# Third attention of a four-layer gated cross-attention program: where VectorE mixes the experts' rows of tiles 3 to 7

## The chip, the core and the metric

The kernel runs on one core of one Trainium2 chip. The metric is the device time of one execution in microseconds (us), from a few executions of the same program; smaller is better. The engines of the core are TensorE (PE in the profile; its weight loads are PEld), VectorE (DVE), ScalarE (ACT), GpSimd (POOL) and SyncE (SP). They run their own instruction streams in order and wait for each other on semaphores.

## What is computed

The input x holds 64 sequences of 64 tokens with 128 features; a context of the same shape goes with it. Four layers follow each other, and each is a gated cross-attention and a gated feed-forward part, both added to x:

```python
x = x + tanh(g_xattn[0]) * L0_xattn(layernorm(x), ctx)
x = x + tanh(g_ffn[0])   * L0_ffn(layernorm(x))             # gated, 384 wide
x = x + tanh(g_xattn[1]) * L1_xattn(layernorm(x), ctx, mask)
x = x + tanh(g_ffn[1])   * L1_ffn(layernorm(x))             # 8 experts, 2 per token
x = x + tanh(g_xattn[2]) * L2_xattn(layernorm(x), ctx)      # the third attention
x = x + tanh(g_ffn[2])   * L2_ffn(layernorm(x))             # block-quantised
x = x + tanh(g_xattn[3]) * L3_xattn(layernorm(x), ctx)
x = x + tanh(g_ffn[3])   * L3_ffn(layernorm(x))             # 4-bit blocks
```

An attention has 16 heads of width 8 over the 64 tokens of its own sequence:

```python
scores = einsum('bhsd,bhtd->bhst', qh, kh) / sqrt(D_K)
attn = softmax(scores, axis=-1)
out = einsum('bhst,bhtd->bhsd', attn, vh)
return out_joined @ W_o + b_o
```

What matters here is the seam between the second feed-forward part and the third attention. The experts' outputs lie in HBM, one row per slot. For each token, the rows of its two experts are gathered, weighted and added to x. Only then can the token be normalised for the third attention.

## The kernel before, in words

**Tiles and halves.** The 4096 tokens are 32 tiles of 128 tokens (two sequences each); tile t = 2i + s is kept with a side s (its parity) and an index i. An attention runs in "halves" (`attention_order`, L55), for t from -3 to 34. Every engine has its own function `half` and runs it for each t in turn. In half t the tiles are in these steps: tile t + 6 is fetched (gathers), tile t + 3 normalised, tile t + 2 turned (its transposition on PE), tile t + 1 gets its key and query, tile t is "new" (scores, row maximum, subtraction, transpositions of the result), tile t - 1 has its probabilities applied to the values, tile t - 2 is divided by its sums and projected by Wo, and the result of tile t - 3 is added to x.

**PE in half t** (L622 to L749): scores of tile t into four PSUM banks (L674), the transposition of normalised tile t + 2 (L640), the one of the output of tile t - 2 (L649), key and query of tile t + 1 (L653, L655), values (L692), probabilities times values for tile t - 1 (L706), the projection (L720, L722), five matmuls of `keep_clock` whose result nobody reads in halves -2, -1 and 0 (L509), and last the eight transpositions of the subtracted scores of tile t (L747), which wait for DVE's two subtractions. ACT takes the exponential (L1038) of what these turn.

**DVE in half t** (L1800 to L1890): the reciprocal of the sums (L1816), the residual of tile t - 3 (L1538), the division (L1827), then `mix` for tile t + 4 in two steps (`scalar_tensor_tensor`, L1570; x += weight times gathered row, once for each expert), the statistics of tile t - 3 (L1837, L1846), the statistics of tile t + 4 (L1852, L1861), the row maximum of tile t over the four banks (L1870), `mixed_eps` for tile t + 4 (L1557), and the subtraction of the maximum in two parts (L1876). `mixed_first` (L66) says that tile t + 4 is mixed so in half t, from half -1 (tile 3) on. The tiles 0, 1 and 2 are mixed ahead of the first half, in a loop of their own (L1996 to L2003). In halves -1 and 0 of the third attention there is nothing but the mixing in front of the row maximum.

**POOL in half t** (L1291 to L1354): it normalises tile t + 3 (L1320), issues the two gathers of tile t + 6 (L1202; from half 0 on behind the scores of tile t), and takes the reciprocal root of the variance of tile t + 4 (L1208, `mixed_rstd`), which waits for DVE's `mixed_eps` of that tile. Its instructions are in order, so whatever stands behind a wait waits too.

The tile's chain is therefore: gathers (POOL, DMA), `mix`, statistics and `mixed_eps` (DVE), root (POOL), normalisation (POOL, in the next half), transposition (PE, in the half after).

## Time and profile before

| | |
|---|---|
| time before, median of 3 runs | 1087.23 us (1087.05 to 1091.18) |
| the profiled execution's own time | 1086.62 us |
| its span, first to last instruction | 1084.8 us |
| busy PE / DVE / ACT / POOL | 901.3 / 885.1 / 686.4 / 523.0 us |
| mean granted TensorE clock | 0.900 of full speed |
| first instruction of the third attention's fetching (POOL) | at 536.66 us |
| row maximum of tile 0 of the third attention | at 555.28 us |
| row maximum of tile 31 of the third attention | at 702.00 us |

Times of rows are microseconds from the start of the span. A row of the timeline has the start, how long it took, the engine, the source line, the operation, what it writes <- what it reads, the shape and how many instructions were merged; in square brackets stands how long the engine was idle before it and who ended that. A PE row shows when a matmul was issued; its end is modelled. The profiled execution is 1.8 us longer than its span, for what lies around it.

### The profile page before, as it was taken

The numbers are of one execution on the slowest core, as the hardware profiler recorded it, in microseconds if no ns is written. First come the engines' busy times: TensorE is split into PE (matmuls) and PEld (weight loads), VectorE is DVE, ScalarE is ACT, GpSimd is POOL, SyncE is SP. The second block draws the span as 40 slices with busy tenths as digits, with TensorE's granted clock in tenths as the row PEclk, the third lists the DMA queues.
The fourth block names the chain that finished last, engine by engine and source line by source line (L and its number), as shares of the span: only waits on it lengthen the run. The fifth ranks groups of instructions, "written<-read, shape, count | busy, mean of one in ns | idle before, by whom it ended". The sixth has DMA issues, their size and how long they took to land.

```text
span 1084.8 us, 30174 instructions
## 1 busy us (share of the span) xinstructions
PE 901.3 (83%) x11571; PEld 708.4 (65%) x11571; DVE 885.1 (82%) x2296; ACT 686.4 (63%) x1794; POOL 523.0 (48%) x612
## 2 busy tenths in 40 slices
PE   8999999999999942899779999978899999434443
PEld 6888889978887731476457778834378888222222
DVE  5998988878899971557568889889978888899997
ACT  5888864377776620354447777866678888555553
POOL 5444402253367676223187877245553332355554
PEclk9999999999999966899899999988999999655665
DMA  8760000000000012456111111000000000000000
GB/s 218 190 232 3 2 3 2 1 2 3 2 22 27 27 43 67 127 174 188 48 34 32 29 30 29 6 1 2 1 2 2 2 3 3 1 10 16 15 15 25
DMA packets 60527, 44.44 MB, mean 41 GB/s; under 512 B 15196, under 2 KB 55781, under 8 KB 59366
## 3 DMA queue, kind: packets, MB, share of 16 engines
q1 hardware_dynamic: 55718, 34.09, 10.8%
q0 software_dynamic: 4096, 8.34, 2.5%
q8 instruction: 91, 1.49, 0.6%
q14 instruction: 46, 0.38, 0.1%
q10 hardware_dynamic: 576, 0.13, 0.1%
HBM read 23.73 MB, written 18.87 MB: 39 GB/s over the span
## 4 chain that ended last, share of the span: by engine, by line
PE 63%; DVE 22%; issue 6%; POOL 5%; DVEq 2%; ACT 2%; DMA 1%; another core or an unknown queue 0%; POOLq 0%; SPq 0%; ACTq 0%
PE ps L747 10%; PE ps L706 9%; PE ps L674 7%; PE ps L586 4%; PE ps L720 4%; PE ps L692 4%; POOL q_out L1232 3%; DVE rowmax L1870 3%; PE ps L791 3%; PE ps L782 3%; PE ps L783 3%; PE ps L640 2%; DVE sm L1876 2%; PE ps L655 2%; PE ps L653 2%
## 5 line engine op out<-in xcount | busy, mean ns | idle before, releaser
L1870 DVE TENSOR_REDUCE rowmax<-ps 128x16 f32<-128x1024 f32 x128 | 155.8, 1217 | 37.2 <-PE ps L674 35.9
L1876 DVE TENSOR_TENSOR sm<-ps,rowmax 128x512 f32<-128x512 f32 x256 | 164.9, 686 | 3.4
L1038 ACT ACTIVATE pr<-ps 128x512 f32<-128x512 f32 x256 | 138.9, 595 | 39.9 <-PE ps L747 37.7
L747 PE MATMUL ps<-cst,sm 128*128 128x128 f32 x1024 | 138.8, 277 | 13.5 <-DVE sm L1876 13.1
L706 PE MATMUL ps<-vbd,pr 128*64 128x18 f32 x4096 | 140.2, 211 | 0.5 <-ACT pr L1038 0.5
L706 PEld LDWEIGHTS ps<-vbd,pr 128*64 128x64 f32 x4096 | 134.2, 138 | 1.3 <-ACT pr L1038 1.3
L1320 POOL TENSOR_SCALAR xn<-x_sb,mv_all,rstd_all 128x128 f32<-128x128 f32 x122 | 98.1, 804 | 72.9 <-PE ps L640 67.0
L747 PEld LDWEIGHTS ps<-cst,sm 128*128 128x128 f32 x1024 | 113.1, 141 | 26.0 <-issue 20.0
L938 ACT ACTIVATE qbd<-ps,bqp,cst 128x128 f32<-128x128 f32 x256 | 104.6, 463 | 5.8 <-PE ps L655 1.9
L975 ACT ACTIVATE vbd<-ps 64x128 f32<-64x128 f32 x256 | 70.8, 277 | 33.9 <-PE ps L692 25.9
L1202 POOL DMA_INDIRECT big<-expert_out,row_g x64 | 68.4, 1068 | 48.5 <-DMA expert_out<-xn_all 23.0
L1218 POOL DMA_INDIRECT slots<-xn_all,row_s x64 | 64.9, 1014 | 35.7 <-DVE sm L1876 17.2
L1232 POOL TENSOR_TENSOR big<-big 128x640 f32<-128x640 f32 (+2 forms) x36 | 39.0, 1106 | 82.8 <-DVE big L1752 62.8
L606 PE MATMUL ps<-ident_b,q_out 128*128 128x128 bf16 x64 | 11.4, 274 | 79.2 <-POOL q_out L1232 79.0
L1194 POOL TENSOR_TENSOR rstd_all<-mv_all,cst 128x1 f32<-128x1 f32 x64 | 36.1, 566 | 78.2 <-DVE mv_all L1855 37.8
L1052 ACT ACTIVATE oT<-ps 128x128 f32<-128x128 f32 x128 | 35.5, 277 | 49.6 <-PE ps L649 48.1
L1208 POOL TENSOR_TENSOR rstd_all<-mv_all,cst 128x1 f32<-128x1 f32 x60 | 34.5, 575 | 63.1 <-DVE mv_all L1849 54.1
L606 PEld LDWEIGHTS ps<-ident_b,q_out 128*128 128x128 bf16 x64 | 4.1, 106 | 92.7 <-POOL q_out L1232 89.4
L720 PE MATMUL ps<-wo,oT 128*128 128x128 f32 x256 | 61.3, 322 | 1.2 <-ACT oT L1052 1.2
L1232 POOL TENSOR_TENSOR q_out<-q_r,q_s 128x1280 bf16<-128x1280 f32 (+2 forms) x18 | 37.9, 2104 | 47.5 <-DVE q_r L1683 44.9
L1538 DVE SCALAR_TENSOR_TENSOR x_sb<-ps,tg,x_sb 128x128 f32<-128x128 f32 x192 | 54.9, 290 | 5.5 <-PE ps L857 3.2
L692 PE MATMUL ps<-wv,ctxT 128*64 128x64 f32 x1024 | 57.9, 234 | 0.1
(296 smaller groups left out, 2351.9 us busy)
## 6 DMA issues: line engine op xcount, KB each, us to landing
slots<-hT SPq DMA_DIRECT2D x8, 1024.0 KB, 12.1
sm<-slots SPq DMA_DIRECT2D x32, 256.0 KB, 3.2
expert_out<-xn_all SPq DMA_DIRECT2D x16, 256.0 KB, 2.9
ew<-in_L_ffn_w SPq DMA_DIRECT2D x24, 128.0 KB, 2.5
out<-x_sb SPq DMA_DIRECT2D x32, 64.0 KB, 1.5
slots<-xn_all,row_s POOLq DMA_INDIRECT x64
big<-expert_out,row_g POOLq DMA_INDIRECT x64
x_sb<-in_x SPq DMA_DIRECT2D x1, 512.0 KB, 4.6
```

Source lines behind the costliest of these rows:

```text
L674: last = nc.tensor.matmul(bank(0, r)[:, b * P:(b + 1) * P], qbd[x][rows, b * S:(b + 1) * S, :].rearrange("d q h -> d (q h)"), kT[x][rows, ...
L692: last = nc.tensor.matmul(dst, ctxT[:, t * P + b * S:t * P + (b + 1) * S], cols, start=True, stop=True, skip_group_check=True)
L706: last = nc.tensor.matmul(dst[:, :, h2, :], probs[:, h2, :], heads[:, :, h2, :], start=True, stop=True, skip_group_check=True)
L720: last = nc.tensor.matmul(mixed[:, M_Y], oT[x][:, :], wo[l][:, :], start=True, stop=(l != 2))
L747: last = nc.tensor.transpose(turned[b][:, r * P:(r + 1) * P], sm[x][:, c:c + P], ident)
L938: nc.scalar.activation(qbd[y][:, :, a], src[:, P:2 * P], ACT.Identity, scale=parity[:, a:a + 1], bias=bqp[l][:, a:a + 1])
L975: last = nc.scalar.activation(dst, src[part, :].rearrange("p (r h w) -> p r h w", h=2, w=HD), ACT.Copy)
L1038: nc.scalar.activation(pr[y][:, b, :], turned[b], ACT.Exp, scale=SCALE).then_inc(p_ready[y], 1)
L1232: return nc.gpsimd.tensor_tensor(dst.rearrange("p (n w) -> p n w", w=width), src.rearrange("p (n w) -> p n w", w=width), factor.unsqueeze( ...
L1320: nc.gpsimd.tensor_scalar(xn[buf][:, :], xt, mv_all[:, 2 * u:2 * u + 1], rstd_all[:, u:u + 1], ALU.subtract, ALU.mult).then_inc(xn_ready[b ...
L1870: v.tensor_reduce(row3, sc, AX.X, ALU.max).then_inc(rowmax_ready[x], 1)
L1876: v.tensor_tensor(sm[x][:, :].rearrange("p (r g k) -> p r g k", r=RG, k=S)[:, part], sc[:, part], row3[:, part].unsqueeze(3).broadcast_to( ...
```

## The change

The mixing of tiles 3 to 7 moves on DVE; the other engines' instructions and their order stay. The loop body for tiles 0 to 2 becomes a function, `mixed_tile(s, i)`: both `mix` steps, a drain, `bn_stats`, a drain, `bn_aggr`, `mixed_eps`. From then on:

- half -1 mixes nothing (it was tile 3);
- halves 0, 1 and 2 mix tile t + 3 (3, 4, 5), behind the row maximum and the subtraction of tile t, where they mixed tile t + 4 ahead of the row maximum;
- half 3 mixes two tiles: tile 6 ahead of its own statistics and row maximum, and tile 7 behind its subtraction;
- from half 4 on everything is as before (tile t + 4, interleaved, ahead of the row maximum).

```diff
+            def mixed_tile(s, i):
+                mix(s, i, 0)
+                mix(s, i, 1)
+                dve.drain()
+                v.bn_stats(bst[1 - s][:, :], x_sb[:, bass.ds((i * NS + s) * D, D)]).then_inc(early_bst[s], 1)
+                dve.drain()
+                v.bn_aggr(mv[1 - s][:, :], bst[1 - s][:, :]).then_inc(early_aggr[s], 1)
+                mixed_eps(s, i)
...
-                    blend = mixed_first(t) if l == 2 else None
+                    blend = mixed_first(t) if l == 2 and t > 3 else None
...
+                    if l == 2 and t == 3:
+                        mixed_tile(0, 3)
                     if blend is not None:
                         mix(x, i, 0)
...
+                    if l == 2 and 0 <= t < 3:
+                        mixed_tile((t + 3) % NS, (t + 3) // NS)
+                    if l == 2 and t == 3:
+                        mixed_tile(1, 3)
...
             for s, i in ((0, 0), (1, 0), (0, 1)):
-                mix(s, i, 0)
...
+                mixed_tile(s, i)
             attention(2)
```

DVE's instructions of halves -1, 0 and 1 of the kernel before (`x_sb<-big` is a `mix` step, `big` holds the gathered rows; `mv<-bst` and `mv_all<-mv` are the statistics and `mixed_eps`; `rowmax` and `sm` are the row maximum and the subtraction):

```order
L1570 SCALAR_TENSOR_TENSOR x_sb<-big,gk,x_sb 128x128 x2
L1852 BN_STATS bst<-x_sb 128x6
L1861 BN_AGGR mv<-bst 128x2
L1557 TENSOR_TENSOR mv_all<-mv,cst 128x2
L1570 SCALAR_TENSOR_TENSOR x_sb<-big,gk,x_sb 128x128 x2
L1852 BN_STATS bst<-x_sb 128x6
L1861 BN_AGGR mv<-bst 128x2
L1870 TENSOR_REDUCE rowmax<-ps 128x16
L1557 TENSOR_TENSOR mv_all<-mv,cst 128x2
L1876 TENSOR_TENSOR sm<-ps,rowmax 128x512 x2
```

and of the changed kernel, halves 0 and 1:

```order
L1881 TENSOR_REDUCE rowmax<-ps 128x16
L1887 TENSOR_TENSOR sm<-ps,rowmax 128x512 x2
L1579 SCALAR_TENSOR_TENSOR x_sb<-big,gk,x_sb 128x128 x2
L1563 BN_STATS bst<-x_sb 128x6
L1565 BN_AGGR mv<-bst 128x2
L1557 TENSOR_TENSOR mv_all<-mv,cst 128x2
L1881 TENSOR_REDUCE rowmax<-ps 128x16
L1887 TENSOR_TENSOR sm<-ps,rowmax 128x512 x2
```

Two mixings (tiles 3 and 4) that stood ahead of the first row maximum now stand behind it. DVE in half 3 of the changed kernel, from its reciprocal on:

```order
L1825 RECIPROCAL rden<-ps 128x16
L1538 SCALAR_TENSOR_TENSOR x_sb<-ps,tg,x_sb 128x128
L1836 TENSOR_TENSOR o_sb<-ps,rden 128x128
L1579 SCALAR_TENSOR_TENSOR x_sb<-big,gk,x_sb 128x128 x2
L1563 BN_STATS bst<-x_sb 128x6
L1565 BN_AGGR mv<-bst 128x2
L1557 TENSOR_TENSOR mv_all<-mv,cst 128x2
L1848 BN_STATS bst<-x_sb 128x6
L1857 BN_AGGR mv_all<-bst 128x2
L1881 TENSOR_REDUCE rowmax<-ps 128x16
L1887 TENSOR_TENSOR sm<-ps,rowmax 128x512 x2
L1579 SCALAR_TENSOR_TENSOR x_sb<-big,gk,x_sb 128x128 x2
```

In this half a whole mixing stands ahead of the row maximum, no longer interleaved with the statistics of tile 0, and a second one behind the subtraction.

## Rows read from the trace of the kernel before

**Rows 1.** The page: busy time of each engine, share of the span, instructions.

```profile
PE 901.3 (83%) x11571; PEld 708.4 (65%) x11571; DVE 885.1 (82%) x2296; ACT 686.4 (63%) x1794; POOL 523.0 (48%) x612
```

**Rows 2.** The timeline of DVE: mixing of tiles 1, 3 and 4, then half 0.

```profile
543.15 0.80 DVE L1570 SCALAR_TENSOR_TENSOR x_sb<-big,gk,x_sb 128x128 f32<-128x128 f32 x2 [0.92 <-DMA big<-expert_out,row_g]
...
544.64 0.16 DVE L1557 TENSOR_TENSOR mv_all<-mv,cst 128x2 f32<-128x2 f32 x1
...
554.08 0.74 DVE L1570 SCALAR_TENSOR_TENSOR x_sb<-big,gk,x_sb 128x128 f32<-128x128 f32 x2 [2.70 <-DMA big<-expert_out,row_g]
...
555.28 1.19 DVE L1870 TENSOR_REDUCE rowmax<-ps 128x16 f32<-128x1024 f32 x1
```

**Rows 3.** The timeline of PE: scores of tile 0 up to those of tile 1.

```profile
551.41 0.73 PE L674 MATMUL ps<-q_r,qbd 32*128 32x128 f32 x16
554.23 0.30 PE L640 MATMUL ps<-cst,xn 128*128 128x128 f32 x1 [2.09 <-POOL xn L1320]
...
555.29 1.25 PE L509 MATMUL ps<-amask,ones_b 128*128 128x512 bf16 x5
557.35 1.16 PE L747 MATMUL ps<-cst,sm 128*128 128x128 f32 x8 [0.80 <-DVE sm L1876]
558.44 0.73 PE L674 MATMUL ps<-q_m,qbd 32*128 32x128 f32 x16
```

**Rows 4.** The timeline of DVE: halves 1 to 3.

```profile
559.75 1.22 DVE L1870 TENSOR_REDUCE rowmax<-ps 128x16 f32<-128x1024 f32 x1 [0.15 <-PE ps L674]
...
561.01 1.29 DVE L1876 TENSOR_TENSOR sm<-ps,rowmax 128x512 f32<-128x512 f32 x2
...
564.66 1.23 DVE L1870 TENSOR_REDUCE rowmax<-ps 128x16 f32<-128x1024 f32 x1 [0.16 <-PE ps L674]
...
569.62 1.22 DVE L1870 TENSOR_REDUCE rowmax<-ps 128x16 f32<-128x1024 f32 x1 [0.62 <-PE ps L674]
```

**Rows 5.** The timeline of PE: end of half 1, and half 2.

```profile
561.85 1.16 PE L747 MATMUL ps<-cst,sm 128*128 128x128 f32 x8 [0.67 <-DVE sm L1876]
562.94 0.73 PE L674 MATMUL ps<-q_r,qbd 32*128 32x128 f32 x16
563.60 0.33 PE L640 MATMUL ps<-cst,xn 128*128 128x128 f32 x1
...
566.76 1.17 PE L747 MATMUL ps<-cst,sm 128*128 128x128 f32 x8 [0.17 <-DVE sm L1876]
```

**Rows 6.** The timeline of POOL: root of tile 3, root and normalisation of tile 4.

```profile
556.77 0.58 POOL L1208 TENSOR_TENSOR rstd_all<-mv_all,cst 128x1 f32<-128x1 f32 x1
...
561.00 0.59 POOL L1208 TENSOR_TENSOR rstd_all<-mv_all,cst 128x1 f32<-128x1 f32 x1
561.69 0.80 POOL L1320 TENSOR_SCALAR xn<-x_sb,mv_all,rstd_all 128x128 f32<-128x128 f32 x1
```

**Rows 7.** The timeline of DVE: halves 4 and 5.

```profile
572.09 0.25 DVE L1816 RECIPROCAL rden<-ps 128x16 f32<-128x16 f32 x1
...
573.88 1.20 DVE L1870 TENSOR_REDUCE rowmax<-ps 128x16 f32<-128x1024 f32 x1
...
577.94 0.26 DVE L1816 RECIPROCAL rden<-ps 128x16 f32<-128x16 f32 x1 [1.53 <-remote]
...
579.82 1.19 DVE L1870 TENSOR_REDUCE rowmax<-ps 128x16 f32<-128x1024 f32 x1
```

**Rows 8.** The timeline of DVE: the block without mixing (half 28), and the maximum of tile 31.

```profile
687.72 0.25 DVE L1816 RECIPROCAL rden<-ps 128x16 f32<-128x16 f32 x1
...
688.58 0.18 DVE L1846 BATCH_NORM_AGGREGATE mv_all<-bst 128x2 f32<-128x6 f32 x1
...
702.00 1.22 DVE L1870 TENSOR_REDUCE rowmax<-ps 128x16 f32<-128x1024 f32 x1 [0.51 <-PE ps L674]
```

**Rows 9.** Two stretches: busy time of PE, PEld, DVE, ACT, POOL; clock, DMA.

```profile
551.00:556.00 5.00, 2.91 (x36) 1.79 (x34) 2.16 (x7) 0.83 (x4) 4.08 (x6) 1.00 0.10 28
561.00:566.00 5.00, 4.33 (x77) 3.70 (x76) 4.27 (x12) 3.59 (x11) 4.29 (x6) 1.00 0.15 41
```

More of the change, by code:

```diff
@@ L1996, in _ @@
             for s, i in ((0, 0), (1, 0), (0, 1)):
-                mix(s, i, 0)
-                mix(s, i, 1)
-                dve.drain()
-                v.bn_stats(bst[1 - s][:, :], x_sb[:, bass.ds((i * NS + s) * D, D)]).then_inc(early_bst[s], 1)
-                dve.drain()
-                v.bn_aggr(mv[1 - s][:, :], bst[1 - s][:, :]).then_inc(early_aggr[s], 1)
-                mixed_eps(s, i)
+                mixed_tile(s, i)
             attention(2)
```

## The prediction

> **What bounds the kernel now.** I read the page first, then the stretch table, then the timelines of DVE, PE and POOL around the start of the third attention, halves -1 to 7. PE is busy 83% of the span and DVE 82% [rows 1]: no engine bounds all of it, so only the place of the change can be judged. The reader is to see three things there.
>
> First, DVE sits in front of the first row maximum without need. The scores of tile 0 are issued at 551.41 [rows 3], but DVE first waits 2.70 us for the gathered rows of tile 4, mixes at 554.08, and starts the maximum at 555.28 [rows 2]. PE then waits 0.80 us for the subtraction, until 557.35 [rows 3]. That wait, not the 2.70 us, is what the start of half 0 costs: PE itself has no use for an earlier subtraction before its five `keep_clock` matmuls end, at 555.29 + 1.25 = 556.54, and these stand behind a transposition that waited 2.09 us for POOL's normalised tile 2 [rows 3].
>
> Second, the halves behind it run in a loop: subtraction, transpositions, scores of the next tile, maximum. Subtraction to transpositions is 0.84 us (561.01 to 561.85), transpositions to scores 1.09 (561.85 to 562.94), scores to maximum 1.31 (558.44 to 559.75) in half 1 and 1.72 (562.94 to 564.66) in half 2, maximum to subtraction 1.26, the subtraction 1.29 [rows 3 to 5]. DVE has little slack in it: 0.15, 0.16 and 0.62 us of waiting for the scores in halves 1 to 3 [rows 4], and it starts the maximum of half 4 at once [rows 7]. In half 5 it waits 1.53 us before its reciprocal [rows 7].
>
> Third, POOL is never late and never idle here: in half 1 its root for tile 4 starts at 561.00 right behind the gathers, and the normalised tile is there at 561.69 + 0.80 = 562.49 [rows 6], 1.1 us before PE turns it at 563.60 [rows 5].
>
> **The change, part by part.** Nothing is added or taken out but the interleaving. A mixing by itself takes 1.65 us, from 543.15 to 544.64 + 0.16 [rows 2]; interleaved with a tile's own statistics the whole block from reciprocal to maximum takes 1.79 (572.09 to 573.88) or 1.88 us (577.94 to 579.82) [rows 7]. The loop for tiles 0 to 2 holds the same instructions as before: nothing, with nothing covering it.
>
> Half 0. The maximum no longer waits for the gather. Scores to maximum is 1.31 in half 1 and 1.72 in half 2 (above); I take 1.31, the nearest. Maximum 552.7, subtraction 554.0 to 555.3. PE finds it ready when `keep_clock` ends, so the transpositions start at about 556.55: **0.8 us earlier**. That is the whole gain; the other 2.2 us of the earlier maximum lie under PE's `keep_clock` and POOL's tile 2. Mixing tile 3 runs 555.3 to 557.0 and POOL's root for it starts at 557.0, not 556.77 [rows 6]: 0.2 us, hidden, since PE turns that tile behind scores that now begin at 557.6.
>
> Half 1. Scores 557.65, maximum 558.95, subtraction 560.2 to 561.5, all 0.8 early. Now tile 4 is mixed from 561.5 to 563.15, where it had been mixed before 555.28. POOL's root for it would start at 561.00 [rows 6] and now waits until 563.15; root and normalisation take 561.00 to 562.49, so tile 4 is normalised at 564.65. Behind this wait on POOL stand only the normalisation of tile 4 and the gathers of tile 7, in the same queue: harmless, since DVE mixes tile 7 only behind half 3's subtraction, 8 us later.
>
> Half 2. PE turns tile 4 at 564.8, against 563.60 [rows 5]: **1.2 us late, and this eats the 0.8**. Its other work up to the transpositions takes what it took, 566.76 - 563.60 = 3.16, so these start at 567.9. DVE: maximum 563.85, subtraction 565.1 to 566.4, mixing of tile 5 until 568.05. Root and normalisation of tile 5 end at 569.55; PE turns it at 569.7, behind the scores of tile 3 (567.9 + 1.09 = 569.0).
>
> Half 3. DVE is free at 568.05. A block without any mixing takes 1.04 us (687.72 to 688.58 + 0.18) [rows 8] and the mixing of tile 6 1.65: maximum at 570.75 against 569.62 [rows 4], 1.1 late. Subtraction 572.0 to 573.3. Tile 7 until 574.95.
>
> Half 4. The block of 1.79 us follows, and DVE's maximum starts at 576.75 against 573.88 [rows 7], 2.9 late; the subtraction ends at 579.3. Here two mixings that used to be done before the first row maximum have been paid inside the loop, with less interleaving.
>
> Half 5. The 1.53 us of DVE's wait in this half [rows 7] take up the rest: block 579.3 to 581.2, against 579.82: **1.4 us late**. The scores of tile 5, behind the subtraction of half 4, are 2.9 late, and what follows them comes at DVE 2.2 late in half 6. From there on each half waits for the one two before it, so the even and the odd tiles carry their own delays, 1.4 and 2.2 us, to the end of the attention. Nothing behind can take them up: the next stage starts when the last tiles are through.
>
> Sum: +1.4 to +2.2, I take +1.8. The profiled execution's own time is 1086.62, so 1088.4; the median of the runs shown is 0.61 above it, so **1089.0 us**. Bounds of what is not known: if scores to maximum is 1.72 in half 0 too, nothing changes (subtraction ends 555.7, still before 556.54). If PE's work in half 2 needs not 3.16 but less, since it has time to catch up during the wait, up to 0.8 comes back. If the block of 1.79 us is lengthened by DVE running against POOL, 0.1 to 0.2 us for each of five tiles comes on top.
>
> A rule weighed here: DVE's `mix` reads two tensors from SBUF while POOL normalises from SBUF. The trace has a mixing of 0.80 us beside a gather's issue and of 0.74 alone [rows 2], so a clash costs 0.06 us and the sum has nothing for it. The Trainium skill (SBUF — State Buffer, Who interferes with whom) says a VectorE instruction with two SBUF inputs and a GpSimd instruction that reads SBUF exclude each other for a whole instruction. By it the sum would be up to +5.8 (rival E); the trace speaks against so much.
>
> **The rivals.**
> (A) The forecast, +0.9 to +2.6: two mixings are paid in a loop without slack. For it: the waits of 0.15 and 0.16 us. Chance 0.53.
> (B) No change, within 0.9: the delays of halves 2 to 4 are taken up by DVE's wait of half 5 and by PE, whose issue runs ahead of its work. For it: after half 5 DVE waits again in every second half. Against: these waits are waits for PE, which is then late itself. Time 1087.2. Chance 0.22.
> (C) Faster: the 0.8 us or more of half 0 is kept. The upper bound is the whole move of the first maximum, 555.28 - (551.41 + 0.73) = 3.1 us [rows 2, 3], so 1084.1; the likely size is the 0.8, so 1086.4. It decides if PE in half 2 doesn't wait for tile 4, that is if DVE's mixing of it ends before 561.9. Chance 0.14.
> (D) Slower by more than can be told from no change, one mechanism: the granted clock of TensorE falls to 1.2 GHz in halves 2 to 4 because PE waits there. Price: PE is busy 4.33 of 5 us in 561 to 566 [rows 9], and up to that much again is added, so 1089.0 + 4.3 = 1093.3. It decides if PE's share of busy time falls below what it was in 551 to 556, 2.91 of 5 us, where the clock stayed at 1.00 (2.4 GHz) [rows 9]; by my timeline it stays above 3.5. The Trainium skill (TensorE: Matmul & The Clock Gate, What's actually happening) names idling as what throttles the array. Chance 0.03.
> (E) DVE's mixing and POOL's normalisation hold each other up: if each of the five moved mixings waited for a whole normalisation of 0.80 us [rows 6], 4.0 us would come on top of 1.8, so +2.6 to +5.8, 1093.0 at most. Against: the 0.80 and 0.74 of rows 2. Chance 0.07. This is where the rule on the SBUF ports, cited above, would lead.
> (F) The change doesn't do what it says. The order of DVE's instructions shows that it does; chance 0.01.
>
> **How the numbers follow.** A measurement of this kernel can tell about 0.5% from no change: 5.4 us. A, B, C and nearly all of E lie within it. The predicted time is A's, 1089.0. The range takes A, B and the likely part of C, down to 1086.0, and the lower part of E up to 1091.5; what is left out is the rest of C, D and the larger half of E, some 0.12, and a margin for the 0.6 us between profile and median. Faster by over 0.5%: 0.01. Slower by over 0.5%: D and the end of E, 0.04. The same: 0.95.
>
> **What would show each step.** In the changed kernel's profile: the maximum of tile 0 about 2.5 us earlier against the scores of tile 0, with no DMA wait of DVE in front; no wait of PE for the subtraction in half 0, and its transpositions right behind `keep_clock`; POOL idle some 2 us in front of its root in half 1, released by DVE; PE waiting for POOL's normalised tile 4 in half 2; DVE without a pause from half 2 to half 5; the distance from the scores of tile 0 [rows 3] to the maximum of tile 31, now 702.00 - 551.41 = 150.6 us [rows 8], at 152.0 to 152.8. It would be wrong if POOL's root doesn't wait in half 1, if DVE idles in halves 3 and 4, or if that distance shrinks.

## The result and the profile after

| | before | changed |
|---|---|---|
| median, 20 runs each | 1089.41 us | 1092.8 us |
| ratio changed / before | | 1.0034, 95% interval 1.0021 to 1.0048 |
| profiled execution, its span | 1086.62, 1084.8 us | 1093.75, 1091.8 us |
| scores of tile 0 to maximum of tile 31 | 150.6 us | 155.3 us |

The change makes the kernel slower by a third of a per cent. That lies within the 0.5% of "no change", but 1092.8 is above the predicted range of 1086.0 to 1091.5. Two of the twenty runs of the changed kernel, of 1703.96 and 2436.44 us, were slow ones: they are in its median and not in the ratio, and the median of the other eighteen is 1091.8 us.

The page of the changed kernel, busy time:

```profile
PE 901.6 (83%) x11553; PEld 709.8 (65%) x11571; DVE 885.8 (81%) x2296; ACT 686.9 (63%) x1794; POOL 524.6 (48%) x612
```

No engine is busy for more than 1.6 us longer than before (POOL, 524.6 against 523.0 [rows 1]): what is lost is lost in waits or in the speed of the clock. DVE's timeline of the changed kernel, the row maxima of tiles 0 to 5 and 31, and two rows between (columns as before: start, duration, engine, line, operation, idle before and its releaser):

```profile
554.20 1.23 DVE L1881 TENSOR_REDUCE rowmax<-ps 128x16 f32<-128x1024 f32 x1 [4.58 <-PE ps L674]
...
556.66 0.73 DVE L1579 SCALAR_TENSOR_TENSOR x_sb<-big,gk,x_sb 128x128 f32<-128x128 f32 x2
...
562.46 1.23 DVE L1881 TENSOR_REDUCE rowmax<-ps 128x16 f32<-128x1024 f32 x1 [4.21 <-PE ps L674]
...
567.12 1.22 DVE L1881 TENSOR_REDUCE rowmax<-ps 128x16 f32<-128x1024 f32 x1
...
572.18 0.26 DVE L1825 RECIPROCAL rden<-ps 128x16 f32<-128x16 f32 x1 [1.02 <-PE ps L722]
...
574.97 1.23 DVE L1881 TENSOR_REDUCE rowmax<-ps 128x16 f32<-128x1024 f32 x1 [0.24 <-PE ps L674]
...
580.74 1.19 DVE L1881 TENSOR_REDUCE rowmax<-ps 128x16 f32<-128x1024 f32 x1
...
585.23 1.19 DVE L1881 TENSOR_REDUCE rowmax<-ps 128x16 f32<-128x1024 f32 x1
...
708.75 1.23 DVE L1881 TENSOR_REDUCE rowmax<-ps 128x16 f32<-128x1024 f32 x1 [0.51 <-PE ps L674]
```

PE's timeline of the changed kernel, halves 0 to 2:

```profile
553.41 0.73 PE L674 MATMUL ps<-q_r,qbd 32*128 32x128 f32 x16
556.24 0.43 PE L640 MATMUL ps<-cst,xn 128*128 128x128 f32 x1 [2.10 <-POOL xn L1320]
...
558.48 1.63 PE L509 MATMUL ps<-amask,ones_b 128*128 128x512 bf16 x4 [0.33 <-issue]
559.94 1.04 PE L747 MATMUL ps<-cst,sm 128*128 128x128 f32 x8
...
564.56 1.16 PE L747 MATMUL ps<-cst,sm 128*128 128x128 f32 x8 [0.89 <-DVE sm L1887]
565.65 0.73 PE L674 MATMUL ps<-q_r,qbd 32*128 32x128 f32 x16
568.41 0.30 PE L640 MATMUL ps<-cst,xn 128*128 128x128 f32 x1 [2.04 <-POOL xn L1320]
...
571.93 1.73 PE L747 MATMUL ps<-cst,sm 128*128 128x128 f32 x8
```

POOL's timeline, the root and the normalisation of tile 4:

```profile
566.79 0.57 POOL L1208 TENSOR_TENSOR rstd_all<-mv_all,cst 128x1 f32<-128x1 f32 x1 [3.94 <-DVE mv_all L1557]
567.47 0.80 POOL L1320 TENSOR_SCALAR xn<-x_sb,mv_all,rstd_all 128x128 f32<-128x128 f32 x1
```

And five stretches (busy time of PE, PEld, DVE, ACT, POOL with the number of instructions, then the granted clock of TensorE as a share of 2.4 GHz):

```profile
core 0: us, PE busy (x) PEld busy (x) DVE busy (x) ACT busy (x) POOL busy (x), PEclk, DMA share, GB/s
...
552.80:556.30 3.50, 1.40 (x21) 0.73 (x19) 2.06 (x3) 0.00 (x0) 2.89 (x5) 1.00 0.15 37
556.30:559.70 3.40, 3.07 (x16) 2.02 (x18) 1.70 (x6) 1.74 (x6) 2.98 (x4) 0.50 0.15 39
559.70:563.10 3.40, 3.40 (x59) 2.89 (x57) 0.64 (x1) 1.95 (x5) 2.67 (x3) 1.00 0.07 19
...
566.50:569.90 3.40, 1.49 (x30) 1.40 (x30) 3.29 (x7) 0.72 (x4) 2.52 (x4) 1.00 0.01 2
569.90:573.30 3.40, 3.40 (x35) 3.36 (x32) 2.09 (x10) 1.91 (x6) 2.76 (x4) 0.50 0.15 39
```

Three things are to be seen. The maximum of tile 0 starts 0.79 us behind the issue of its scores (554.20 against 553.41; before 3.87 behind). POOL's root of tile 4 waits 3.94 us for DVE, and PE then waits 2.04 us for that tile. And twice the clock falls to 0.50, that is 1.2 GHz, for 3.4 us: the eight transpositions of half 2 take 1.73 us instead of 1.17 [rows 5], and in half 0 the four `keep_clock` matmuls that this profile has of the five take 1.63 us where five took 1.25 [rows 3]. Just before each fall lies a stretch in which PE did little: 1.40 of 3.50 and 1.49 of 3.40 us. In the profile of the kernel before, the clock stays up. Its stretches ahead of tile 0's scores (issued at 551.41), around PE's wait in half 0 (552.14 to 554.23), and where PE turns tile 4 (563.60):

```profile
546.30:549.70 3.40, 1.57 (x9) 0.90 (x7) 0.84 (x4) 1.78 (x5) 2.97 (x4) 1.00 0.13 39
549.70:553.10 3.40, 2.04 (x22) 1.08 (x22) 1.34 (x5) 0.28 (x1) 2.89 (x4) 1.00 0.08 22
553.10:556.50 3.40, 2.27 (x18) 1.31 (x18) 2.32 (x6) 1.33 (x5) 2.81 (x4) 1.00 0.13 39
...
563.30:566.70 3.40, 3.29 (x66) 2.83 (x58) 3.14 (x8) 2.20 (x8) 2.91 (x4) 1.00 0.14 39
```

PE's wait in half 0 is the same in both kernels (2.09 and 2.10 us), and so are PE's instructions up to its end; cut so that it holds the whole wait, the stretch from 550.8 to 554.3 of the kernel before has PE busy for 1.41 of 3.50 us, at a clock of 1.00. So the first fall can't be put down to the change, and before2, below, has such a fall without it. The wait ahead of the second one, 2.04 us for tile 4, is: the kernel before has none there.

So there were two candidates: the order itself (the late tile 4 and the mixings inside the loop), and the clock. The experiments take them apart.

### The profile page after: what moved, and what is told of

Read it like the earlier page. It is cut to its first block, busy times and chain, and to the rows that moved or that the text cites. A ratio compares the mean times of both kernels' runs of the same rounds, so it can differ in the third digit from the quotient of the medians.

```text
span 1091.8 us, 30166 instructions
## 1 busy us (share of the span) xinstructions
PE 901.6 (83%) x11553; PEld 709.8 (65%) x11571; DVE 885.8 (81%) x2296; ACT 686.9 (63%) x1794; POOL 524.6 (48%) x612
## 3 DMA queue, kind: packets, MB, share of 16 engines
q0 software_dynamic: 4096, 8.34, 2.6%
HBM read 23.73 MB, written 18.87 MB: 39 GB/s over the span
## 4 chain that ended last, share of the span: by engine, by line
PE 61%; DVE 23%; issue 7%; POOL 5%; DVEq 2%; ACT 1%; DMA 1%; another core or an unknown queue 0%; POOLq 0%; SPq 0%; ACTq 0%
PE ps L747 9%; PE ps L706 9%; PE ps L674 6%; PE ps L586 4%; PE ps L720 4%; PE ps L692 3%; DVE rowmax L1881 3%; PE ps L782 3%; PE ps L791 3%; PE ps L783 3%; POOL q_out L1232 2%; PE ps L640 2%; DVE sm L1887 2%; PE ps L655 2%; PE ps L653 2%
```

## The experiments

Every kernel was timed in turns with the kernel before on the same chip. Most ran on chips on which the kernel before takes 1072 to 1074 us ("faster chip" below), three (one4, late4_fill2, two2) on one where it takes 1088, about as on the first ("slower chip"). Halves are shorter on the faster chip (4.3 us against 4.7, from half 5 to half 31), so lengths are compared at one speed only. Here is all of it; "maxima" are the starts of the row maxima of halves 1 to 5 behind the first matmul of tile 0's scores in the same profile, "length" is that of tile 31's, and "1.2 GHz" lists each stretch at that clock between the two, as duration at its start.

| kernel | ratio, 95% interval | maxima 1 to 5 | length | 1.2 GHz |
|---|---|---|---|---|
| faster chip | | | | |
| before2 | 0.9994, 0.9983 to 1.0005 | 8.60 12.75 17.13 21.86 26.09 | 138.8 | 3.4 at 4.3 |
| b_fill0 | 0.9997, 0.9984 to 1.0011 | 8.06 12.93 17.15 21.71 26.01 | 138.7 | none |
| after2 | 1.0030, 1.0017 to 1.0043 | 6.94 11.60 18.26 24.00 28.25 | 140.9 | none |
| after3 | 1.0015, 1.0001 to 1.0029 | 8.36 13.02 21.78 27.64 31.87 | 144.6 | 3.4 at 4.5, 6.8 at 14.7 |
| a_fill2 | 1.0020, 1.0005 to 1.0035 | 6.95 11.61 18.28 24.02 28.28 | 141.0 | none |
| a_fill02 | 1.0008, 0.9991 to 1.0024 | 6.93 11.59 18.26 24.00 28.25 | 140.6 | none |
| after3_fill02 | 1.0007, 0.9994 to 1.0020 | 6.93 11.59 18.26 24.00 28.25 | 140.9 | none |
| two0 | 1.0001, 0.9989 to 1.0013 | 6.95 11.40 16.32 22.15 26.38 | 139.5 | none |
| two0tb | 1.0010, 0.9999 to 1.0021 | 8.01 12.34 16.57 21.47 25.70 | 139.4 | none |
| late4 | 1.0038, 1.0024 to 1.0053 | 8.60 14.23 22.29 26.84 31.13 | 143.7 | 10.2 at 11.9 |
| late4_fill2b | 1.0039, 1.0022 to 1.0056 | 8.87 14.50 20.61 25.37 29.60 | 142.6 | 3.4 at 11.6 |
| one4_fill1 | 0.9999, 0.9987 to 1.0011 | 8.45 13.10 17.34 22.20 26.42 | 139.0 | none |
| slower chip | | | | |
| before (first profile) | | 8.34 13.25 18.21 22.47 28.41 | 150.6 | none |
| changed (first profile) | 1.0034, 1.0021 to 1.0048 | 9.05 13.71 21.56 27.33 31.83 | 155.3 | 3.4 at 2.9, 3.4 at 16.5 |
| two2 | 1.0023, 1.0011 to 1.0034 | 6.94 11.60 18.87 24.33 28.59 | 152.2 | none |
| one4 | 1.0015, 1.0002 to 1.0029 | 8.48 13.30 20.04 25.40 29.78 | 152.0 | 6.8 at 12.0 |
| late4 once more (late4_fill2) | 1.0044, 1.0029 to 1.0060 | 8.59 14.22 22.29 27.85 32.23 | 154.5 | 10.2 at 11.9 |

### Both kernels again

before2 and after2, and after3 later, are the two kernels unchanged.

> The kernel before once more, for a profile of it on the same chip as the experiments, where its runs come 15 us lower than on the first one. Expected: the same time as the kernel before beside it; row maxima of the third attention some 4.3 us apart as in the experiments so far, not 4.8, with no waiting of DVE between them; 138 to 139.5 us from the scores of tile 0 to the maximum of tile 31.

> The changed kernel once more, on this chip. Theory 1 (PE's wait for tile 4 plus a fall of the granted clock behind it): PE waits 1.5 to 2.5 us in half 2, the clock falls to 1.2 GHz in at least one stretch between half 0 and half 4, and the time is 2.5 to 5 us above the kernel before; with the eight unread matmuls it was +2.1. Rival (all of it is the order of DVE's work): +2.1 us as with the matmuls.

> The changed kernel again, beside its filled version on the same chip. Both theories: ratio 1.002 to 1.0045. The profile tells whether the clock falls in halves 0 to 4 on this chip in that execution: with a fall the attention takes 154 to 155.5 us (143 on the faster chip), without one 152.2 to 153 (140.9).

The kernel before gives its own time again (0.9994). The changed one gives 1.0030 and 1.0015. Its two profiles at this speed differ: in after2 the clock stays at 2.4 GHz and the attention takes 140.9 us, in after3 it falls twice and the attention takes 144.6. The program is the same; one execution loses 3.7 us more in the attention than the other, and the maxima part where the clock falls (halves 1 and 3). Of the twelve runs of each, after2's profiled one was the fastest (1073.07 us) and after3's the slowest (1078.00). The kernel before is not free of it either: in before2's profile the clock falls for 3.4 us in half 0 and its maximum of half 1 stands at 8.60, where b_fill0, with the clock up, has 8.06. So the order by itself costs 140.9 - 138.8 = 2.1 us of the attention, and a fall comes on top in some executions. The four profiles of this order with the clock up (after2 and the three with filling, below) have 140.6 to 141.0 us.

### Matmuls where PE waits

The changed kernel with eight more `keep_clock` matmuls behind the scores, in half 2 (a_fill2) or in halves 0 and 2 (a_fill02, after3_fill02); b_fill0 is the kernel before with them in half 0.

```diff
                         last.then_inc(s_psum[x], 1)
+                    if l == 2 and t in (0, 2):
+                        keep_clock(8)
```

> The changed kernel, with eight unread matmuls of 512 columns on PE in half 2, behind the scores of tile 2 and ahead of the transposition that waits for POOL's normalised tile 4. Nothing else differs. Theory 1 (the loss has two parts: PE's wait for tile 4, worth 1.2 to 2 us, and the granted clock that falls to 1.2 GHz behind that wait, worth up to 3.4 us more): the wait stays, the clock stays at 1.00 from half 1 to the end of the attention, and the time comes down from +3.7 us over the kernel before to +1.5 to +2.5. Rival (the clock falls by chance, and the whole loss is the order of DVE's work): the time stays at +3 to +4.5 us.

> The kernel before, with eight unread matmuls of 512 columns on PE in half 0, behind the scores of tile 0 and ahead of the transposition that waits for POOL's normalised tile 2. In both kernels PE waits 2.1 us there. If that wait lets the clock fall in some executions of either kernel (it fell at 556.3 in the changed kernel's profile and not in that of before), the spread of the runs shrinks and the median falls by 0.5 to 2 us; if the clock has nothing to do with it, median and spread stay as they are.

> The changed kernel with the eight unread matmuls in half 0 and in half 2. Theory 1: the clock holds at 1.00 through the whole third attention in every profile, and what is left over the kernel before with the same filling in half 0 is the order of the work alone: +1.2 to +2.2 us. Rival: +3 us or more is left.

> The changed kernel with eight keep_clock matmuls each in halves 0 and 2. If the clock's fall is in the changed kernel's median, this is faster than it by 1 to 3 us: ratio 1.0005 to 1.002, no stretch at 1.2 GHz in the attention, length 152.2 to 153 (140.6 on the faster chip). If the order alone makes the loss, the ratio equals that of the changed kernel within 0.001.

Stretches of after3, the changed kernel, ahead of its second fall and in it:

```profile
557.38:560.78 3.40, 1.39 (x23) 1.04 (x22) 2.92 (x8) 1.23 (x3) 1.72 (x3) 1.00 0.02 4
560.78:564.18 3.40, 3.40 (x47) 3.13 (x46) 2.11 (x7) 2.35 (x8) 2.63 (x4) 0.50 0.15 39
564.18:567.58 3.40, 3.40 (x28) 3.04 (x27) 2.27 (x10) 1.24 (x3) 2.90 (x4) 0.50 0.06 19
```

and of after3_fill02, run beside it, at the same place (its half 2):

```profile
558.30:561.70 3.40, 3.35 (x49) 2.22 (x47) 3.30 (x7) 0.97 (x4) 2.81 (x4) 1.00 0.01 2
561.70:565.10 3.40, 3.18 (x46) 2.82 (x42) 2.84 (x13) 2.78 (x8) 2.76 (x4) 1.00 0.16 39
```

With the wait filled, PE is busy 3.35 of 3.40 us where it was busy 1.39, and the clock stays at 1.00. None of the three filled profiles has a fall in the attention; of the three without filling two have it (changed, after3) and one has not (after2). The medians go down, by 1075.18 - 1073.38 = 1.8 us for after3 and after3_fill02, which were timed together, and the ratios from 1.0030 (after2) to 1.0020 and 1.0008 (a_fill2, a_fill02, timed at another time). The intervals overlap: that a fall comes in some executions and what it costs there is shown, while its share in the median is only indicated, at 1 to 2.5 us. The kernel before gains nothing from them in half 0 (0.9997). What the order costs is seen best here, with the clock out of it. DVE's timeline of after3_fill02, the maxima of tiles 0, 3, 4, 5 and 31, the end of tile 5's mixing with the first row of half 3, and one mixing:

```profile
547.79 1.23 DVE L1883 TENSOR_REDUCE rowmax<-ps 128x16 f32<-128x1024 f32 x1 [4.38 <-PE ps L674]
...
562.46 0.16 DVE L1559 TENSOR_TENSOR mv_all<-mv,cst 128x2 f32<-128x2 f32 x1
562.72 0.26 DVE L1827 RECIPROCAL rden<-ps 128x16 f32<-128x16 f32 x1
...
563.26 0.80 DVE L1581 SCALAR_TENSOR_TENSOR x_sb<-big,gk,x_sb 128x128 f32<-128x128 f32 x2
...
565.26 1.19 DVE L1883 TENSOR_REDUCE rowmax<-ps 128x16 f32<-128x1024 f32 x1
...
570.99 1.19 DVE L1883 TENSOR_REDUCE rowmax<-ps 128x16 f32<-128x1024 f32 x1
...
575.25 1.19 DVE L1883 TENSOR_REDUCE rowmax<-ps 128x16 f32<-128x1024 f32 x1
...
687.89 1.23 DVE L1883 TENSOR_REDUCE rowmax<-ps 128x16 f32<-128x1024 f32 x1 [0.51 <-PE ps L674]
```

and POOL's of the same kernel:

```profile
558.26 0.57 POOL L1210 TENSOR_TENSOR rstd_all<-mv_all,cst 128x1 f32<-128x1 f32 x1 [1.84 <-DVE mv_all L1559]
...
563.38 0.90 POOL L1322 TENSOR_SCALAR xn<-x_sb,mv_all,rstd_all 128x128 f32<-128x128 f32 x1
```

and PE's, which turns tile 4 and then transposes the scores of half 2:

```profile
559.88 0.30 PE L640 MATMUL ps<-cst,xn 128*128 128x128 f32 x1
...
562.52 1.04 PE L749 MATMUL ps<-cst,sm 128*128 128x128 f32 x8
```

Against b_fill0, whose clock stays up as well, the filled kernel is 1.1 us early in half 1 (6.93 against 8.06), 1.1 late in half 3, 2.3 late in half 4 and 2.2 in half 5 and at tile 31 (140.9 against 138.7). The late tile 4 has little part in that: DVE ends the mixing of tile 5 at 562.46 + 0.16 = 562.62 and starts half 3 at 562.72, so PE holds it up by 0.10 us at most (as much in after2, where nothing fills PE's wait of 1.88 us). What makes half 3 late is that DVE itself is busy without a pause, with tile 5 behind the subtraction of half 2 and tile 6 ahead of the maximum of half 3.

### Where tile 4 is mixed

two0tb and late4 mix tile 3 behind half 0's subtraction and tiles 5, 6, ... interleaved ahead of the maximum, as before; they differ in tile 4 alone.

Against the changed kernel, in two0tb:

```diff
-                    blend = mixed_first(t) if l == 2 and t > 3 else None
+                    blend = mixed_first(t) if l == 2 and t > 0 else None
...
+                    if l == 2 and t == 0:
+                        mixed_tile(1, 1)
+                        mixed_tile(0, 2)
```

and in late4, with the same `blend`:

```diff
+                    if l == 2 and t in (0, 1):
+                        mixed_tile((t + 3) % NS, (t + 3) // NS)
```

> Tiles 3 and 4 are both mixed behind the subtraction of half 0, where DVE has nothing else; from half 1 (tile 5) on everything is as in the kernel before. So no mixing is added to DVE's loop of halves 1 to 5 and no tile comes late. If DVE's loop and tile 4's lateness are the whole loss, this keeps what half 0 gains: maximum of tile 1 at 7.8 us behind the scores of tile 0 against 8.1 to 8.3, and a time 0 to 0.8 us below the kernel before. If the early maximum itself does harm, it is above it.

> Tile 3 is mixed behind the subtraction of half 0 and tile 4 behind that of half 1, as in the changed kernel; tiles 5 and on as in the kernel before, interleaved and ahead of the row maximum. This takes out what the change does in halves 2 and 3. If tile 4's lateness (POOL's root waits, PE waits for the tile) is most of the loss: +1.5 to +4 us, with PE waiting 1.5 us or more in half 2. If the two whole mixings of half 3 are most of it: 0 to +1.

> Tile 3 behind half 0's subtraction, tile 4 behind half 1's, the rest as in the kernel before, plus eight keep_clock matmuls in half 2 behind the scores. Without them: 1.0038 and 1.0044, clock at 1.2 GHz for 10.2 us from 11.9. If the clock makes most of it: no such stretch in the attention, length about 2 us shorter (about 141.5 on the faster chip, 152.5 on the slower), ratio 1.001 to 1.0025. If the order makes it, ratio 1.0035 or more.

The one tile moved by one half takes the ratio from 1.0010 to 1.0038, by 0.0028 or 3.0 us. POOL's and PE's timelines of late4:

```profile
562.10 0.57 POOL L1208 TENSOR_TENSOR rstd_all<-mv_all,cst 128x1 f32<-128x1 f32 x1 [3.28 <-DVE mv_all L1557]
```

```profile
563.82 0.45 PE L640 MATMUL ps<-cst,xn 128*128 128x128 f32 x1 [1.54 <-POOL xn L1320]
```

In two0tb no root of POOL waits there and PE turns tile 4 without a pause. But this is not where late4's loss begins. With only tile 3 to mix in half 0, DVE comes early to tile 5 and waits 2.56 us for its rows (0.34 us in two0tb); the maximum of tile 1 starts at 8.60 instead of 8.01, PE waits 1.66 us for that subtraction instead of 1.06, and the clock falls at 11.9, ahead of PE's wait for tile 4. The first outcome in late4_fill2b's expectation, that the clock makes most of it, did not come: with eight matmuls in half 2 the stretch at 1.2 GHz shrinks from 10.2 to 3.4 us and the attention from 143.7 to 142.6, and PE no longer waits for tile 4, but the ratio stays at 1.0039, 1.0022 to 1.0056. The matmuls stand in half 2, and the fall that is left begins ahead of them, behind PE's wait of 1.93 us for the subtraction of half 1. So the pair two0tb and late4 shows what the whole chain costs, the wait for tile 5's rows and the fall included; what a late tile 4 costs by itself it does not show. The kernel that ran under the name late4_fill2 did not have the matmuls that its expectation speaks of: it was late4 once more, on the slower chip, and repeats it (1.0044 after 1.0038).

> The order with tile 3 behind half 0's subtraction and tile 4 behind half 1's (143.7 us, ratio 1.0038, clock at 1.2 GHz for 10.2 us from 11.9) with eight keep_clock matmuls in half 2 behind the scores. If the fallen clock makes what that kernel loses beyond the changed one without a fall (140.9), no stretch at 1.2 GHz shows within the attention, the length is 140.5 to 141.5 and the ratio 1.001 to 1.002. If the late tile 4 and the order cost it by themselves, the length stays above 143 and the ratio at 1.003 or more.

### Other places for the mixings

two0 is the changed kernel with tile 4 mixed behind half 0's subtraction too, and tiles 5, 6, 7 behind those of halves 1, 2, 3, so that tiles 4, 5 and 6 are mixed one half earlier and half 3 has one mixing instead of two.

```diff
-                    if l == 2 and t == 3:
-                        mixed_tile(0, 3)
...
-                    if l == 2 and 0 <= t < 3:
-                        mixed_tile((t + 3) % NS, (t + 3) // NS)
-                    if l == 2 and t == 3:
-                        mixed_tile(1, 3)
+                    if l == 2 and t == 0:
+                        mixed_tile(1, 1)
+                    if l == 2 and 0 <= t < 4:
+                        mixed_tile((t + 4) % NS, (t + 4) // NS)
```

> As the changed kernel, but tiles 3 and 4 are both mixed behind the subtraction of half 0, tile 5 behind that of half 1, 6 of half 2 and 7 of half 3, so that every tile from 4 on is mixed one half earlier. Theory 1 (tile 4 is normalised too late because it is mixed behind the subtraction of half 1): POOL's root for tile 4 no longer waits, PE doesn't wait in half 2, the clock doesn't fall there, and the time is 0 to 1 us below the kernel before. Rival (two mixings more inside DVE's loop are what costs): DVE has the same work in halves 0 to 3 as the changed kernel less one tile, and the time stays 1 to 3 us above the kernel before.

The wait for tile 4 is gone, the halves 1 to 3 stay 0.8 to 1.5 us ahead of b_fill0 (6.95, 11.40, 16.32 against 8.06, 12.93, 17.15), and the kernel is as fast as the one before. But the lead is lost from half 3 to half 4 (16.32 to 22.15), where the last mixing behind a subtraction is followed at once by the first interleaved one: two mixings between two maxima. Whoever moves work behind the maximum has to pay that once.

two2 puts tile 6 behind tile 5 in half 2, and tile 7 where it was in the kernel before:

```diff
-                    blend = mixed_first(t) if l == 2 and t > 3 else None
+                    blend = mixed_first(t) if l == 2 and t > 2 else None
...
-                    if l == 2 and t == 3:
-                        mixed_tile(0, 3)
...
-                    if l == 2 and t == 3:
-                        mixed_tile(1, 3)
+                    if l == 2 and t == 2:
+                        mixed_tile(0, 3)
```

> The changed kernel with tile 6 mixed behind half 2's subtraction too (after tile 5), and tile 7 interleaved ahead of the maximum of half 3, as in the kernel before. The changed kernel's length without a fall of the clock is 140.9 on this chip, the kernel before's 138.8. If the two mixings of half 3 (one of them in front of its maximum) make the +1.1 there and most of what stays, the cost only moves here, since half 2 now has two: maxima of halves 3 and 4 as late, length 140.5 to 141.5, ratio 1.002 to 1.003. If it is tile 4, late in half 1, that costs by itself, the same. If only the uninterleaved block of half 3 costs, the length is 139.5 to 140 and the ratio 1.000 to 1.001.

1.0023, and 152.2 us with the clock up: the cost only moves. That excludes the third reading of the expectation, that the uninterleaved block of half 3 alone costs; the first two foretold the same, so two2 does not tell between them. The double mixing now lies between the maxima of halves 2 and 3 (11.60 to 18.87; before 13.25 to 18.21).

one4 moves tile 4 alone, behind half 0's subtraction, and leaves tile 3 in half -1; one4_fill1 adds four `keep_clock` matmuls in half 1.

```diff
-                    blend = mixed_first(t) if l == 2 and t > 3 else None
+                    blend = mixed_first(t) if l == 2 and t != 0 else None
...
-                    if l == 2 and t == 3:
-                        mixed_tile(0, 3)
...
-                    if l == 2 and 0 <= t < 3:
-                        mixed_tile((t + 3) % NS, (t + 3) // NS)
-                    if l == 2 and t == 3:
-                        mixed_tile(1, 3)
+                    if l == 2 and t == 0:
+                        mixed_tile(0, 2)
```

> Only tile 4's mixing moves: behind the subtraction of half 0; tile 3 is mixed in half -1, and tiles 5 to 7 interleaved ahead of the maximum, as in the kernel before. On this chip the third attention of the kernel before takes 138.8 us from the scores of tile 0 to the maximum of tile 31, with the second maximum at 8.1 to 8.6. If half 0's gain is real and what loses it is that tile 4 comes late and that several mixings are paid inside the loop, this order keeps it: second maximum at about 6.9 to 7.5, length 137.6 to 138.3, ratio 0.999 to 1.000. If the loop of PE absorbs any early start by itself (as in the kernel with tiles 3 and 4 behind half 0's subtraction, 139.4), the length is 138.8 to 139.4 and the ratio 1.000 to 1.001.

> Only tile 4's mixing behind half 0's subtraction, plus four keep_clock matmuls in half 1 behind the scores. Without them the attention took 152.0 us in the profile, with the clock at 1.2 GHz for 6.8 us from 12.0 us behind the scores of tile 0, PE busy 2.19 of the 3.4 us in front of that, and the ratio was 1.0015. If the fall alone made it slower than the kernel before, it is gone here: no stretch at 1.2 GHz in the attention, third and fourth maximum at about 13.3 and 18 instead of 13.3 and 20.0, length about 150 to 150.6 (before 150.6) on a chip of that speed or 138 to 139 on the faster one, ratio 0.999 to 1.000. If the order costs by itself, length 151.5 or more (139.5 or more) and ratio 1.001 or more.

DVE's timeline of one4, its mixing of tile 5 ahead of the maximum of half 1:

```profile
557.51 0.74 DVE L1579 SCALAR_TENSOR_TENSOR x_sb<-big,gk,x_sb 128x128 f32<-128x128 f32 x2 [2.41 <-DMA big<-expert_out,row_g]
...
558.72 1.19 DVE L1879 TENSOR_REDUCE rowmax<-ps 128x16 f32<-128x1024 f32 x1
```

and POOL's, which issued the gathers of tile 5 in between:

```profile
552.24 0.80 POOL L1320 TENSOR_SCALAR xn<-x_sb,mv_all,rstd_all 128x128 f32<-128x128 f32 x1
553.22 1.13 POOL L1202 DMA_INDIRECT big<-expert_out,row_g  x1 [0.18 <-issue]
554.66 1.00 POOL L1202 DMA_INDIRECT big<-expert_out,row_g  x1 [0.31 <-issue]
555.69 0.58 POOL L1208 TENSOR_TENSOR rstd_all<-mv_all,cst 128x1 f32<-128x1 f32 x1
556.38 0.80 POOL L1320 TENSOR_SCALAR xn<-x_sb,mv_all,rstd_all 128x128 f32<-128x128 f32 x1
```

With tile 4 out of its way, DVE waits as long for the rows of tile 5 in half 1 (2.41 us) as it did for those of tile 4 in half 0 (2.70 [rows 2]): POOL, which does not pause, brings one tile in 556.38 - 552.24 = 4.14 us, and whoever starts earlier waits for it in the next half. PE then waits 1.21 us for the subtraction of half 1, the clock falls for 6.8 us, and the kernel is slower than before (1.0015, on the slower chip). With the four matmuls, on the faster chip, there is no fall and the ratio is 0.9999; their intervals overlap. None of the kernels tried beats the one before.

## Why the prediction was wrong, and where it was right

**The base.** The forecast was 1.8 us over the kernel before; the ratio says 3.7 (0.0034 x 1089.4), with an interval of 2.3 to 5.2. That the change loses, and by an amount of this kind, was forecast. But the predicted time lay 3.8 us under the measured one, and 2.2 us of that is the base: I started from 1087.23, the median of three runs, and twenty runs of the same kernel have 1089.41. "a margin for the 0.6 us between profile and median" in the range was too small for three runs. Another 1.0 us is the step from the median of all twenty runs, 1092.8, to that of the eighteen in the ratio, 1091.8. The latter is 2.4 us over the kernel before, 0.6 more than forecast.

**Half 0.** "0.8 us earlier. That is the whole gain" was right in kind. The maximum starts 0.79 us behind the scores (I took 1.31), PE does not wait for the subtraction, and the transpositions stand right behind `keep_clock`. ("The other 2.2 us" was a slip: 555.28 - 552.7 = 2.6 us less 0.8 leaves 1.8.) With the clock up, half 1 is 1.1 us ahead (6.93 against 8.06), a little more than I said. In the changed kernel's first profile the fall in half 0 ate it: 9.05 against 8.34.

**Halves 1 and 2.** "POOL's root for it would start at 561.00 and now waits until 563.15" was right. The wait measures 1.84 us without a fall, and 3.26 (after3) and 3.94 with one. PE waits for tile 4: 1.88 us in after2, 2.01 in after3, 2.04 in the first profile. "This eats the 0.8" was wrong as to what eats it. The "3.16" of PE's work behind tile 4 was too long, 562.52 - 559.88 = 2.64 us in after3_fill02, and the late tile holds DVE up by 0.10 us only, as long as the clock stays up.

**Halves 3 to 5.** I had +1.1, +2.9 and +1.4 us, and then 1.4 and 2.2 by turns to the end. With the clock up, on the faster chip, +1.1, +2.3 and +2.2 were measured, and +2.2 at the end; there the kernel before has no wait of DVE in half 5 that could take anything up. On the slower chip, for which the forecast was made, the one profile of the changed kernel has falls, but two2, with the same order up to the mixing of tile 5, has none: its halves 3 to 9 are +0.7, +1.9, +0.2, +1.7, +0.9, +1.7 and +0.9 us against the kernel before. The changed kernel's own, on top of its falls, go from +4.9 in half 4 to +3.4 in half 5, where DVE waits 0.17 us ahead of its reciprocal instead of 1.53. So "The 1.53 us of DVE's wait in this half take up the rest" was right there, and so were the two delays that take turns. They do not last: from half 11 on every tile has the larger one, 1.6 to 1.7 us in two2 and 4.4 to 5.0 in the changed kernel. The distance to the maximum of tile 31 was to be 1.4 to 2.2 us longer; with the clock up it is 2.1 to 2.2 on the faster chip and 1.6 in two2, and 4.7 in the first profile. "DVE without a pause from half 2 to half 5" holds with the clock up (0.23 us at most in after3_fill02) and fails in the first profile (1.02 us in half 3), where DVE waits for a PE at 1.2 GHz.

**The clock.** This is the step that failed: the sum has no term for it, and rival D had a chance of 0.03, because PE's busy share "by my timeline ... stays above 3.5" of 5 us. My own timeline had PE idle from 562.9 (subtraction 560.2 + 0.84 + 1.09 + 0.73) to 564.8 in half 2 and I didn't add it up. Measured were 2.96 of 5 us (565 to 570) in the first profile and 2.83 (555.8 to 560.8) in after3, and within these 1.49 and 1.39 of 3.40. In place of a steady clock came a fall to 1.2 GHz in two of the changed kernel's three profiles, worth 3.7 us with that of half 0 (after3 against after3_fill02): 1.4 of them are there by half 2 (13.02 against 11.59), so some 2.3 belong to the fall behind the wait for tile 4. The 4.3 that I had as its bound holds. The criterion was no good either: the clock fell with 2.96 of 5 us, above the 2.91 of rows 9, and behind 2.19 of 3.40 in one4, and stayed up with 1.41 of 3.50 in half 0 of the kernel before. The runs of the first comparison point the same way. Eight of the changed kernel's eighteen took 1093.8 to 1098.5 us, longer than any of the kernel before (1093.64 at most), at a mean clock over the program of 0.893 against 0.899 in the other ten, which took 1089.0 to 1091.8; in which stage they lost it was not recorded. So what came is A and D together, D in part of the executions. I had treated D as a rival where the fall of half 2 was a consequence of A: an engine made to wait 2 us in a place where it had little else. The fall of half 0 was not; the kernel before has it too, in before2. The Trainium skill (TensorE: Matmul & The Clock Gate, What's actually happening) says that the throttled state is the default and activity lifts it; the filled kernels agree, 3.35 of 3.40 us busy and a clock of 1.00.

**The rivals B, C and E.** B (PE and DVE's waits take it up) fails in the attention by 140.9 against 138.7. C was right that the early maximum is worth something and wrong that it stays: it needed tile 4 mixed before 561.9, and that was at 566.55 (558.01 - 546.99 = 11.0 us behind the scores in after3_fill02, where 561.9 is 10.5) - and two0, which meets this condition, keeps the lead for three halves only. For E, after3_fill02 has a mixing and a normalisation at the same time: 0.80 us instead of 0.73, and 0.90 instead of 0.80. The clash costs 0.07 and 0.10 us there, not a whole instruction, and not every time: in the profile of the kernel before, 25 of the 31 normalisations that follow the first mixing run beside one, at a median of 0.80 us as the other six, 0.96 at most. The lower of the two readings that I weighed was right, though its evidence was misread: the mixing of 0.74 us at 554.08 was not alone either, since POOL issued a gather from 554.26 on.

**What stays open.** The filled kernels lose 2.1 us in the attention by their profiles but only 0.8 us (0.0007 x 1073) in their medians, with an interval up to 2.1. The other part may lie behind the attention, where the clock falls in every profile, first for 6.8 to 17.1 us, and the stage then takes 93.2 to 96.4 us to the first maximum of the next attention. The longer that first fall, the longer the stage: 93.2 to 94.7 us behind 6.8, 94.5 to 95.2 behind 10.2, 95.4 to 96.0 behind 13.7, 96.4 behind 17.1. Attention and this stage together take 140.9 + 93.2 = 234.1 us in after2 and in after3_fill02, 138.8 + 94.5 = 233.3 in before2 and 138.7 + 95.8 = 234.5 in b_fill0, so in these profiles the 2.1 us are largely gone behind the stage. Whether that is chance or a consequence of the later end, one profile of each does not settle. Nor is it shown why the clock of the same kernel falls in one execution and not in another.

## What to carry to other kernels

Work taken out of the front of a software pipeline has to be paid inside its loop; if the loop has no slack, the gain at the front lives only until the first half that holds two of the moved pieces. Before moving a producer behind something, follow its whole chain (here mixing, root, normalisation, transposition): tiles 3 and 4 behind the first subtraction cost nothing that the runs can tell (1.0010, 0.9999 to 1.0021), and tile 4 one half later took it to 1.0038, with the wait for rows and the fall of the clock that came with it. And wherever a forecast gives TensorE a wait of 2 us that it did not have, add up its busy time around it and give a fall of the clock a term and a real chance, since the fall can cost more (3.7 us here) than the wait (0.10 us of delay here with the clock up).

## What was not expected of the hardware

- The same program, with the same instructions, ran its third attention in 140.9 us and in 144.6 us; what sets the two profiles apart is 10.2 us at 1.2 GHz. A single profile of such a kernel is no measure of the order of its instructions.
- Stretches with PE busy 1.57 of 3.40 us and 1.41 of 3.50 kept their clock in the kernel before; one with 1.49 of 3.40 (changed) and even one with 2.19 (one4) were followed by a fall. Rows of one4:

```profile
558.80:562.20 3.40, 2.19 (x37) 1.76 (x36) 2.89 (x6) 2.49 (x7) 3.10 (x4) 1.00 0.17 43
562.20:565.60 3.40, 3.40 (x48) 2.95 (x42) 3.24 (x8) 1.67 (x7) 2.82 (x4) 0.50 0.15 39
```

- A fall is handed on, but did not grow: in half 0 of the changed kernel it moved the maximum of tile 1 from 6.94 to 8.36 (after3) and 9.05 us (first profile), and the wait of POOL's root grew by as much, from 1.84 to 3.26 and 3.94 us, while PE's own wait for tile 4 stayed at 1.88 to 2.04 us.
